# Four changes to a four-layer graph network kernel: step one's message table by VectorE from PSUM, early border matrices, layer one's last five waves in one turn, and the final norm on rows

## What is computed

```python
# L0, four steps: gated graph network
m = (embedding @ W_msg.T + b_msg).reshape(n, N_EDGE_TYPES, DIM)
q = m[src, etype]
r = jax.ops.segment_sum(q, dst, num_segments=n)
embedding = _gru_cell(r, embedding, w_ih, w_hh, b_ih, b_hh)
# L1: message passing with an edge network
pe = jax.nn.relu(edge_w @ pos_w1) @ pos_w2
msg = pe * x[src] + x[src]          # summed by dst, divided by the count
out = relu(batchnorm(concatenate([x, agg]) @ sage_w + sage_b)) + x
# L2: one more gated step, with an embedding of the edge type
# L3: attention over edges, then
h = graphnorm(x + x_att)
return h + gelu(h @ W1 + b1, approximate=False) @ W2 + b2
# and the last line of all
x = _layernorm(x + L3(x))
```

## Time and profile before

| what | value |
|---|---|
| three runs | 4305.17, 4314.5, 4315.24 us (median 4314.5) |
| the profiled execution | 4308.27 us |
| its span | 4306.1 us |
| TensorE busy | 2866.4 us (67%) |
| GpSimd busy | 2773.2 us (64%) |
| VectorE busy | 1810.6 us (42%) |
| ScalarE busy | 947.5 us (22%) |
| mean granted TensorE clock | 0.819 |

### The profile page before, as it was taken

How to read it: one execution, slowest core, us unless ns; L and a number is a source line. 1 busy time by engine, 2 the same in 40 slices (tenths; PEclk the granted TensorE clock), 3 DMA queues, 4 the chain that set the end, 5 groups by cost and what they waited for, 6 DMA issues and landing times. The chain is left out here.

```text
span 4306.1 us, 51197 instructions
## 1 busy us (share of the span) xinstructions
PE 2866.4 (67%) x12128; PEld 2161.1 (50%) x12129; DVE 1810.6 (42%) x4815; ACT 947.5 (22%) x3063; POOL 2773.2 (64%) x2899
## 2 busy tenths in 40 slices
PE   6555585556756558666677787775566766664697
PEld 3444444444444444444446676544444456554574
DVE  5222252222522225444463333422222766667874
ACT  4111131111311113111122222321111211111334
POOL 5777767777677776777737777367776377774000
PEclk9777797776977779787789999977777888887799
DMA  4212222121211122112212112111111245453340
GB/s 167 53 53 52 53 87 52 52 52 52 87 52 52 52 52 87 52 52 53 52 36 63 52 53 53 28 52 52 52 52 45 65 153 157 153 157 107 108 147 15
DMA packets 141570, 308.74 MB, mean 72 GB/s; under 512 B 48723, under 2 KB 63258, under 8 KB 140986
## 3 DMA queue, kind: packets, MB, share of 16 engines
q0 software_dynamic: 95040, 208.45, 17.9%
q1 hardware_dynamic: 46458, 99.48, 6.7%
HBM read 246.11 MB, written 61.63 MB: 71 GB/s over the span
## 5 line engine op out<-in xcount | busy, mean ns | idle before, releaser
L635 POOL DMA_INDIRECT ring<-m_tab,idx x1564 | 1487.4, 951 | 505.4 <-issue 475.1
L1668 PE MATMUL ps<-nodes,ring 128*128 128x256 f32 (+1 forms) x2776 | 876.0, 480 | 495.3 <-DMA ring<-m_tab,idx 372.8
L1668 PE MATMUL ps<-oh,ring 128*128 128x256 f32 (+1 forms) x2814 | 876.8, 475 | 472.2 <-DMA ring<-m_tab,idx 367.9
L757 ACT ACTIVATE ring<-ring 128x128 f32 x2346 | 506.1, 295 | 2244.8 <-DMA ring<-m_tab,idx 1566.5
L1668 PEld LDWEIGHTS ps<-nodes,ring 128*128 128x128 f32 x2776 | 630.2, 250 | 642.0 <-issue 537.7
L1668 PEld LDWEIGHTS ps<-oh,ring 128*128 128x128 f32 x2814 | 632.9, 248 | 618.9 <-issue 504.7
L635 POOL DMA_INDIRECT ring<-x_tab,idx x782 | 741.4, 948 | 247.2 <-issue 235.9
L1137 DVE TENSOR_SCALAR oh<-iota,dl 128x256 f32<-128x256 f32 x1200 | 367.9, 377 | 921.8 <-PE ps L1668 921.3
L1137 DVE TENSOR_SCALAR nodes<-iota,dl 128x256 f32<-128x256 f32 x1180 | 358.3, 374 | 840.8 <-PE ps L1668 840.6
L635 POOL DMA_INDIRECT ring<-kv_tab,idx x416 | 405.6, 975 | 133.3 <-issue 126.4
L645 POOL TENSOR_TENSOR small<-small,bc 128x4 f32<-128x4 f32 (+1 forms) x28 | 29.6, 1056 | 471.2 <-DVE small L1244 469.2
(11 more groups left out here) (280 smaller groups left out, 2661.1 us busy)
## 6 DMA issues: line engine op xcount, KB each, us to landing
ve_dr<-pw SPq DMA_DIRECT2D x52, 512.0 KB, 3.0
ring<-ve_dr SPq DMA_DIRECT2D x52, 512.0 KB, 3.4
ring<-m_tab,idx POOLq DMA_INDIRECT x1564, 2.5
m_tab<-ring SPq DMA_DIRECT2D x75, 256.0 KB, 2.1
ring<-x_tab,idx POOLq DMA_INDIRECT x782, 2.5
ring<-kv_tab,idx POOLq DMA_INDIRECT x416
nodes<-in_xT SPq DMA_DIRECT2D x2, 1600.0 KB, 13.5
kv_tab<-nodes SPq DMA_DIRECT2D x25, 128.0 KB, 1.7
```

What stands on the lines that cost most here:

```text
L635: pool.indirect_dma_start(rows[:, j, :], None, table, bass.IndirectOffsetOnAxis(ap=idx[:, wave * WV + j:wave * WV + j + 1], axis=0)).then_ ...
L757: ins = nc.scalar.activation(ring_flat[:, ds(r[j], P)], rows[:, j, :], ACT.Copy)
L1668: return T.matmul(o, lhsT, rhs, start=start, stop=stop, skip_group_check=True)
```

## The change

**One.** The 25 table matmuls stand first on TensorE and wait only for their PSUM bank. VectorE adds the bias straight from PSUM into `first_buf`, all 25 tiles, and only then starts the index work at `w_dst`. ScalarE's copies and GpSimd's adds are gone. `i_4` is computed before the table (for the 391 tiles), so that gathers wait for it and for the table, and no longer for `i_1`. `w_dst` uses a piece of `pw`, since gathers may now fill `ring`.

**Two.** The one-hot matrices of wave 50 wait for one credit less where no types are counted.

**Three.** In layer one the loop has 11 turns, and waves 44 to 48 are one turn written out; the last waves use the same extra buffers as in other passes (`END_HALVES`), border matrices don't wait for credits, and a bank is evacuated when its own border matmuls are done.

**Four.** The final norm works on rows: `rest` adds bias, `hT` and `xT` ahead of the matmuls' end, one addition from PSUM makes `yT`, TensorE transposes it (`turn_y`), and VectorE takes statistics per window of 128 rows from PSUM (`rows_stats`), GpSimd the power, and VectorE subtracts and multiplies from PSUM into `tb` (`rows_scaled`).

```diff
-            for n in range(BY_POOL):
-                pool.wait_ge(mt_ac, n + 1)
-                nc.gpsimd.tensor_tensor(first_buf[n], first_buf[n], brow[:, 0:512], ALU.add).then_inc(mt_pb, 1)
-            pool.wait_ge(s_dv, DV["i_1"])
+            pool.wait_ge(s_dv, DV["i_4"])
+            pool.wait_ge(s_ac, AC["r_a10"])
...
-            act.wait_ge(s_dv, DV["w_dst"])
-            for n in range(WIN):
-                act.wait_ge(in_mm, n + 1)
-                nc.scalar.activation(first_buf[n], ps[:, 4 + n % RING, :], ACT.Copy).then_inc(mt_ac, 1)
...
+            step("i_4", V.scalar_tensor_tensor(idx4[:, 0:TILES], R[:, :, F_SRC], float(ET), R[:, :, F_T4],
+                                               ALU.mult, ALU.add))
+            for n in range(WIN):
+                dve.wait_ge(in_mm, n + 1)
+                V.tensor_tensor(first_buf[n], ps[:, 4 + n % RING, :], brow[:, 0:512], ALU.add).then_inc(mt_vb, 1)
...
-                    dve.wait_ge(credit, wave_no(k, i, u) + DEPTH - bufs + 1)
-                    ins = pair_hot(k, u, g, n)
+                    beyond = isinstance(g, int) and g > M_WAVES
+                    dve.wait_ge(credit, wave_no(k, i, u) + DEPTH - bufs + (0 if beyond and not counting else 1))
+                    ins = pair_hot(u, g, n)
...
-            if c == NCH - 1 or l1(k):
+            if c == NCH - 1:
                 eng.wait_ge(credit, first_wave(k + 1) + DEPTH)
...
-            with eng.Fori(0, LOOPED) as i:
+            with eng.Fori(0, LOOPED - 1) as i:
                 turn(i, [i * DEPTH + u for u in range(DEPTH)])
-            turn(LOOPED, list(range(LOOPED * DEPTH, M_WAVES)))
+            turn(LOOPED - 1, list(range((LOOPED - 1) * DEPTH, M_WAVES)))
...
             for wave in range(M_WAVES + 1, P_WAVES):
-                dve.wait_ge(credit, first_wave(PASS_L1) + DEPTH + wave - 1)
-                pair_hot(PASS_L1, wave - LOOPED * DEPTH, wave, tiles_of(wave)).then_inc(oh_ready, 1)
+                pair_hot(wave - LOOPED * DEPTH, wave, tiles_of(wave)).then_inc(oh_ready, 1)
...
-            for c in range(NCH + 3):
-                norm(3, c - 1, lambda c: None)
+            def rows_stats(c):
+
+                nw = CH[c][1] // P
+                dve.wait_ge(ln_t, NCH * OUTS[3] + c + 1)
+                for w_ in range(nw):
+                    step(f"ys{c}_{w_}", V.bn_stats(y_st(c, w_), ps[:, 4 + c % 4, w_ * P:(w_ + 1) * P]))
+                if c >= 2:
+                    dve.wait_ge(ln_o, NCH * OUTS[3] + c - 1)
+                for w_ in range(nw):
+                    after(f"ys{c}_{w_}")
+                    step(f"ya{c}_{w_}", V.bn_aggr(y_mv(c)[:, w_, :], y_st(c, w_)))
+                after(f"ya{c}_{nw - 1}")
+                V.tensor_scalar(y_ve(c), y_mv(c)[:, 0:nw, 1], EPS, None, ALU.add).then_inc(ln_s, 1)
...
+            def rows_scaled(c):
+
+                nw, b = CH[c][1] // P, c % 2
+                dve.wait_ge(ln_r, NCH * 3 + c + 1)
+                if c >= 2:
+                    dve.wait_ge(ln_dma[b], LN_DMA(3, b) + 16 * (c // 2))
+                for w_ in range(nw):
+                    ins = V.tensor_scalar(tb[:, b, w_ * P:(w_ + 1) * P], ps[:, 4 + c % 4, w_ * P:(w_ + 1) * P],
+                                          y_mv(c)[:, w_, 0:1], y_rs(c)[:, w_:w_ + 1], ALU.subtract, ALU.mult)
+                ins.then_inc(ln_o, 1)
+
+            rest(0)
+            for c in range(NCH + 2):
+                if c + 1 < NCH:
+                    rest(c + 1)
                 if c < NCH:
                     c0, cw = CH[c]
                     dve.wait_ge(s_pe, PE[f"ffo{c}_3"])
...
+                    after(f"hx{c}")
+                    V.tensor_tensor(yT[:, c0:c0 + cw], yT[:, c0:c0 + cw], ps[:, 3, 0:cw], ALU.add).then_inc(ln_y, 1)
+                if 1 <= c <= NCH:
+                    rows_stats(c - 1)
+                if c >= 2:
+                    rows_scaled(c - 2)
```

More of the change, by code:

```diff
@@ L675, in _ @@
             nc.gpsimd.tensor_copy(alE[:, TILES + EXTRA:SLOTS, :], alE[:, 0:SLOTS - TILES - EXTRA, :]).then_inc(ex_x, 1)
-            norm(3)
+            for c in range(NCH):
+                pool.wait_ge(ln_s, NCH * 3 + c + 1)
+                nc.gpsimd.tensor_tensor(y_rs(c), y_ve(c), b_("minus_half").to_broadcast([P, CH[c][1] // P]),
+                                        ALU.pow).then_inc(ln_r, 1)
         @block.scalar
@@ L926, in _ @@
                                                     bias=small[:, 5:6], scale=small[:, 4:5]))
-            for c in range(NCH + 4):
-                for j in range(4 if c < NCH else 0):
+            for c in range(NCH):
+                for j in range(4):
                     cw = CH[c][1]
@@ L1085, in _ @@
             after("x_last")
-            step("i_4", V.scalar_tensor_tensor(idx4[:, :], rec[:, :, F_SRC], float(ET), rec[:, :, F_T4],
-                                               ALU.mult, ALU.add))
             step("i_1", V.tensor_copy(idx1[:, :], rec[:, :, F_SRC]))
@@ L1266, in norm_alone @@
                     scaled(ln, c - 1)
-            for n in range(BY_POOL, WIN):
-                dve.wait_ge(mt_ac, n + 1)
-                V.tensor_tensor(first_buf[n], first_buf[n], brow[:, 0:512], ALU.add).then_inc(mt_vb, 1)
             dT = pw[:, 0, :]
@@ L1644, in _, with rest @@
             step("gn_shift", V.tensor_tensor(small[:, 5:6], b_("L3_gn_b"), small[:, 7:8], ALU.subtract))
-            for c in range(NCH + 3):
-                norm(3, c - 1, lambda c: None)
+            def rest(c):
+                c0, cw = CH[c]
+                dve.wait_ge(s_ac, AC[f"gn{c}"])
+                step(f"hx{c}", V.scalar_tensor_tensor(yT[:, c0:c0 + cw], hT[:, c0:c0 + cw], b_("L3_b2"),
+                                                      xT[:, c0:c0 + cw], ALU.add, ALU.add))
+            def rows_stats(c):
[23 more added lines that the diff above has]
+                    rest(c + 1)
                 if c < NCH:
@@ L1735, in borders @@
                     pe.wait_ge(moved, k * P_EXTRA + b0 + j + 1)
-                    ins = mm(psf[:, c0:c0 + PAIR], border_rows(b0 + j), pair_oh(k, u, wave, j), start=False, stop=False)
+                    ins = mm(psf[:, c0:c0 + PAIR], border_rows(b0 + j), pair_oh(u, wave, j), start=False, stop=False)
                     if (b0 + j) % 2 == 0:
@@ L1910, in scatter @@
                         ins = mm(psf[:, ds(c0[4 * h + j], PAIR)], wave_rows(waves[u], u)[:, 4 * h + j, :],
-                                 pair_oh(PASS_L1, u, waves[u], 4 * h + j), start=False, stop=False)
+                                 pair_oh(u, waves[u], 4 * h + j), start=False, stop=False)
                     return ins
@@ L2108, in _, with turn_y @@
                 mm(ps[:, 2 + b, 0:cw], wbeta[:, 1, :], wk[:, 0, b, 0:cw], start=False).then_inc(f_b, 1)
+            def turn_y(c):
+                c0, cw = CH[c]
+                pe.wait_ge(ln_y, NCH * 3 + c + 1)
+                if c >= 4:
+                    pe.wait_ge(ln_o, NCH * OUTS[3] + c - 3)
+                for j in range(cw // P):
+                    ins = T.transpose(ps[:, 4 + c % 4, j * P:(j + 1) * P], yT[:, c0 + j * P:c0 + (j + 1) * P], ident)
+                ins.then_inc(ln_t, 1)
             for k in range(4 * NCH + 2):
@@ L2126, in _ @@
                                            stop=(j == 3)))
-                    if j == 1:
-                        norm(3, c - 1)
-            for c in range(NCH - 1, NCH + 3):
-                norm(3, c)
+                    if j == 1 and c:
+                        turn_y(c - 1)
+            turn_y(NCH - 1)
 GRU_COLS = [f"{L}_{n}" for L in ("L0", "L2") for n in ("bih_r", "bih_z", "bin", "bhh_r", "bhh_z", "bhn")]
```

54 lines of the change are left out of this document (25 added, 29 removed).

## The result

| | kernel before | changed kernel |
|---|---|---|
| runs of the first measurement | 4305.17, 4314.5, 4315.24, 4305.64 us | 4261.16, 4273.42, 4267.83, 4265.46 us |
| median | 4310.07 us | 4266.65 us |
| ratio to before, 95% interval | | 0.9904 (0.989 to 0.9918) |
| the same measured once more (six runs against eleven) | 4311.39 us | 4268.66 us, ratio 0.9908 (0.9891 to 0.9925) |
| profiled execution, its span | 4308.27, 4306.1 us | 4261.16, 4259.2 us |

The change makes the kernel 40 to 43 us faster. The forecast was 4279 (4263 to 4294), 31 us under the 4310.07 of the now four runs of the kernel before; sign, range and places were right, and the gain was some 10 us larger than the sum of 32.2.

A forecast was written before the change was run, and what follows sets the result against it. GpSimd's indirect gathers were taken as the bound, the edits touching what lies between passes. Gains 10 + 5.4 + 5.8 + 11 = 32.2 us off the profiled 4308.3 gave 4276, set at 4279 towards the median; range 4263 to 4294.

The forecast's parts named there:

- The table: Opening: 25 tiles from about 16.3, 3.5 of them slow and 21.5 at 0.86 us, ending near 41.7.
- The index work: Opening: VectorE's index operations now follow the table and take 17.9 us, so `i_dl` ends at 59.6.
- 52 transposes and their evacuation, all of it about 9.5, `dT` and two copies, 1.6: Opening, after `i_dl`: these steps put the first hidden matmul at 70.7, against 71.26 before.
- The last term: Opening: from the first hidden matmul to the first credit 22.4 us as before, so the credit comes at 93.1.
- The doubt about a crawl: Opening: VectorE's index work might run as slowly beside gathers as beside GpSimd's adds; called the largest doubt.
- speaks against it for the gathers: Opening: the earlier trace was read as showing no blocking of VectorE's index operations behind gathers, unlike behind adds.
- half of it: Layer one: the boundary before wave 44 may turn cold, 1.7 us worse; half, 0.9 us, was deducted.
- The small operations: Last stage: VectorE's 128-column stats, aggregates and scalings, taken at 0.25 us each; at 0.5 the norm gains 3 us.
- gathers crawl: Opening: index work slow beside gathers, first credit near 100, table edit gives 3 us: 4286; chance 0.13.
- part 1 gives nothing: Opening and tail: first credit after 103.5 and small operations at 0.5 us, 14 us in all, 4297; chance 0.08.
- the clock in layer one: Layer one: clock stays low through the first wave of each turn, 77 us slower, 4356; chance 0.02.
- Milder boundaries in layer one: Layer one: a different phase makes most cold loop boundaries mild, worth 5 us more, 4274; chance 0.09.

The follow-up runs named there:

- the run with longer index work: Two fills on VectorE (3200 and 1536 columns) put ahead of the index work, against the changed kernel: 4272.62 us, ratio 0.9914.
- the repeated profile: The changed kernel measured and profiled once more, nothing edited: 4268.66 us, ratio 0.9908 to the kernel before.
- the run with the banks together: Layer one's banks evacuated only after the last border matmul again, against the changed kernel: 4272.74 us, ratio 0.9913.
- both runs with early hidden matmuls: Changed kernel with 11 of step one's hidden matmuls before the transposes: 4266.75 us; also with counting-step copies first and nine waves in layer one's last turn: 4255.68 us.

## Why the prediction was right, and where it was off

The mechanism held at all four places, and every part gave more than forecast. Two parts lie above their own bounds: the opening (13.85 us against 13) and the border matrices (4 x 1.86 = 7.4 against 6). The sum of the bounds was also added up wrongly: gains of 15 to 40 us under the profiled 4308.3 are 4268 to 4293, where the text has 4264 to 4293. On the base of 4311 that the forecast uses they are 4271 to 4296, and the measured 4266.65 lies below that. The stated range held it because it reached down to 4263.

**The opening** (forecast 10, bounds 6 to 13; measured 13.85 at the pause's end, 103.56 to 89.71, and 12 to 15 at step two's first gather in the run of this part alone). The reasoning held step by step, and two of its terms were too large. The table: fewer slow tiles (from the third addition on they are 0.86 us apart), so the last addition ended at 40.60 where 41.7 was forecast, though an addition took 0.69 and not 0.61, hidden behind TensorE's 0.86. The index work: 40.60 to 58.34 is 17.7, forecast 17.9. The term that was mis-sized most is "52 transposes and their evacuation, all of it about 9.5, `dT` and two copies, 1.6": the stretch from `i_dl` to the first hidden matmul took 67.22 - 58.34 = 8.9 and not 11.1. The 52 transposes took 7.24 us, 0.14 each, at a granted clock of 0.81; the forecast had started from 6.85 us for 36, a row with a clock of 0.59. The last term, 22.4 to the pause's end, was 22.49.

The doubt about a crawl is settled for VectorE. The copy took 0.22 us, and three 128x403 operations, 1.3 to 1.5 us beside the additions, took 0.4 to 0.6; a fourth (0.97 before) took 0.85. The Trainium skill (SBUF — State Buffer, "Who interferes with whom") calls the port pair that VectorE and GpSimd share an exclusive lock, which GpSimd needs for the writing of descriptors too (this last the section marks as inferred). This trace agrees for GpSimd's additions. It shows no blocking of VectorE by gathers in these operations. But it shows the other side: gathers beside the index work got longer. In the changed kernel the copy stands between two gathers; in the run with longer index work it stands inside one, keeps its 0.21 us, and the gather takes 1.28 instead of 0.94:

```profile
64.70 1.28 POOL L642 DMA_INDIRECT ring<-m_tab,idx  x1 [0.30 <-issue]
65.12 0.21 DVE L1106 COPY iota<-cst 128x128 f32<-128x128 f32 x1
```

Six of the changed kernel's first 32 gathers, besides the very first, took 1.07 to 1.49 us (two took 1.09 and 1.17 before), and the 32 took 41.57 us from first to last against 40.25 before. The pause of 4.24 us hides this, and so does the mean over 1564 gathers, 951 ns as in the earlier trace rows. The forecast's "speaks against it for the gathers" is thus right for VectorE's rows alone. That the two wait for the same port is not tested by any run here.

**Early border matrices** (forecast 1.35 a pass, 5.4 in all; measured 1.86 a step and 6.5 us alone). Right in kind, and small in size: from wave 48's last matmuls to wave 49's it was 3.00 us before (554.06 to 557.06, with the 1.44 of the earlier trace rows in it) and is 1.40 now, so 1.60 went there; another 0.1 went behind it, to the hidden state's next matmuls (5.29 us before, 5.18 now). The last 0.15 of the 1.86 is not placed.

**Layer one** (forecast 5.8, bounds 3 to 8; measured 7.8 in the trace, 7.5 between the groups). The boundary at 48 gave 3.1, not 3.6 (wave 44 to 48: 40.97 before, 37.86 now). In the first profile the boundary at 44 did become a long one, 1.76 and not half of it, but earlier boundaries fell 2.2 better, which is chance; in the repeated profile it stayed short (6.68 us between two multiplies, against 8.36), so "half of it" was a fair guess. The wait before wave 49 and the wait for all banks gave 12.24 - 8.83 = 3.4, forecast 3.1. The term that was missing: with the banks evacuated one by one, the transposes behind the first also start earlier, another 0.8 to 0.9 us, shown by the run with the banks together.

**The final norm** (forecast 11, bounds 3 to 13; measured 11.3 and 12.0 in the two profiles). Chunks 7.49 us apart, forecast 7.53. The small operations were the part without a row: statistics 0.22, aggregate 0.09, scaling 0.34 us, against 0.25 for each. From y5 to the last scaling it took 8.8 us, forecast 9.6. Counted from y0, the first of the L1650 and L1690 rows, to the end of the span it is 60.4 us before and 48.3 and 48.4 now, 12.0 in both profiles.

**What belongs to no part.** Of the 47 us between the two profiled executions, up to 3 are the clock in layer two and 1.6 the clock in the counting step, where three of wave 49's matmul pairs took 1.20 us before and 0.68 after. The profiled run of the changed kernel is also its fastest of four. The forecast of 31 on the median stands against 40 to 43: +3.9 for the opening, +2 for layer one, +1 to 2 for the borders, up to 1 for the norm, and the rest inside the intervals.

The rivals: gathers crawl, part 1 gives nothing, and the clock in layer one are refuted by the rows above. Milder boundaries in layer one did not come with the change (seven long ones among twelve boundaries before, seven among eleven after), but came by chance in one run, with 531.06.

## What to carry to other kernels

When two waits stand behind one resource, here the table and the credit for the gathers, compute both times; the later one prices the edit, and the gap between them is what the next edit may win. Where GpSimd's arithmetic is moved away, some of VectorE's own operations beside it get several times faster (1.24 to 0.22 us) and others don't (0.87 and 0.84 at `i_dl`), so price each from rows beside the new neighbour, and look at what the neighbour loses too. And where a pass's time scatters by several us from run to run, judge an edit of a few us by its place in the trace, not by the median.

## What the runs showed that was not expected

A delay and what came of it were not of one length: 5.04 us on VectorE became 7.84 at the gathers, since TensorE's clock was lower in the transposes (8.60 us for 7.48) and in the first scatter (5.41 for 3.72). That the delay did this is not shown: the transposes came after the same idle time as before (10.29 and 10.35 us), and the first scatter took 5.35 us in a run without the delay. It took 5.41 in both runs with early hidden matmuls too, where the 52 transposes themselves took only 5.92. So one profile doesn't price a delay of this kind to within 3 us.

The lower clock moves about. The same ten matmuls of layer two took 4.56 us in six profiles and 6.0 to 7.6 in eight, with nothing changed near them. Layer one's pass scattered by 8 us with one order of work, with three to nine of its boundaries at the lower clock. What decides at which boundaries the clock falls was not tried and stays open.
